# A two-layer graph network with expert FFNs on one core: a list of tile sizes for each layer, and first-layer edge sums placed over 27 of 32 FFN steps

## The chip, the cores and the metric

One core of a Trainium2 chip. The metric is the device time of one execution in microseconds, taken as the median of three runs. One more execution was profiled, and every row below is from it.

## The reference, cut to what matters

There are 6250 nodes of 256 features and 106250 edges sorted by destination node (50000 pairs in both directions and a loop at each node). Four residual steps follow each other:

```python
x = x + gnn0(layernorm(x), edge_weight1)   # mean over in-edges of w*feat[src], [mean, feat] @ W.T + b
x = x + ffn0(layernorm(x))                 # 8 experts, 512 hidden, ReLU, the best 2 by logit
x = x + gnn1(layernorm(x), edge_weight)    # h = relu(xn @ Wp.T + bp); sqrt(sum of w*h[src]**2)
x = x + ffn1(layernorm(x))                 # 8 experts, 256 hidden, GELU, top 2 of a softmax, plus the normed x
```

All four steps are per node, except that each GNN reads rows of arbitrary other nodes. So the first "layer" of the kernel (gnn0 and ffn0) must be through with every node before the second (gnn1 and ffn1) gathers its first row.

## The kernel before, in words

**Tiles.** Nodes are cut into 49 blocks of 128, and the blocks into tiles. `Shape` (line 38) makes one list for both layers: eleven tiles of 4 blocks, then 2, 2 and 1, so 14 tiles. All FFN work of a tile has its 512 (or 256, 128) nodes as the moving columns of the matmul.

**Groups.** Edges come in 208 groups of 512. For a group GpSimd issues four indirect DMAs (L574, `gather_group`), each of which fetches 128 source rows into a ring of SBUF buffers; the ring holds 4 groups in layer 0 and 8 in layer 1, and the gather of group g waits until group g-4 (g-8) has been summed. VectorE makes the one-hot matrices of the group (`onehots`, L1061, L1062; in layer 1 L1066, L1067), TensorE multiplies rows and one-hots into a window of PSUM (`sum_groups`: in layer 0 24 matmuls of L649 and 4 of L653, in layer 1 8 records of L657), and VectorE adds the window to an accumulator in SBUF (`add_windows`, L1091). A tile can be "taken" from the accumulator (`take`) when all its groups have been added. `END[t]` is the number of groups that must be there for tile t; for a full tile there are 17 new ones. The first tile needs 19 groups.

**FFN steps.** A tile goes through M steps, 32 in layer 0 (8 experts of 4 chunks of 128 hidden units) and 16 in layer 1 (8 of 2). Step n on TensorE: `up(n+2)` (6 matmuls, L667), `down(n)` (6 matmuls, L697), and then what is woven in. ScalarE applies the activation (L1432) and makes the high half (L1439), VectorE scales (L1250) and makes the low half (`hidden_low`, L1255, exactly once in each step of each layer, 672 in all). `down(n)` waits for the low half of step n, and in a step with groups also for their one-hots and for the windows of the groups before.

**What is woven in.** At fixed steps of tile t: the results of tile t-1 go back to tokens and, in layer 0, to the table of layer 1 (steps 1 to 12), and tile t+1 is prepared. In layer 0 that is `take` from step 13, features (13), the linear product (18, 19), layernorm and transposes (22), gate logits (24), and the combine weights (29), which `down` waits for in step 30. In layer 1 the same stands at 1, 3, 4, 7, 9 and 13.

**Where the sums go.** `plan` (line 346) writes for each step the groups that are summed in it. The groups of tile t go partly into the last steps of tile t-2, from step `turn` on, and partly into the first `at_take` steps of tile t-1. In layer 0 `turn` is 28 and `at_take` is 13:

```python
early = len(gs) * (self.M - self.turn) // self.M      # 17 * 4 // 32 = 2
late = gs[early:]                                     # 15
```

So in a full tile of layer 0 two groups are summed in steps 28 and 30, fifteen in steps 0 to 12, and none in steps 13 to 27. In layer 1 (`turn` 1, `at_take` 1) one is summed in each of steps 1 to 15 and two in step 0. The groups between the first tile's and the first step's (`begun`) are summed in four places of the first tile's preparation.

**The start of a layer.** GpSimd gathers the groups of tile 0, VectorE finds the largest weight of each matrix between them (`magnitudes`, `at_mags`), GpSimd reduces these over partitions (ahead of group 10), VectorE computes the scales (group 10 in layer 0, 8 in layer 1), and in the groups after these the 16 weight matrices are split into a high and a low half, by ScalarE (L1444) and VectorE (L1003) in turn. Then the tile is taken and prepared, and the first step begins. Layer 1's gathers begin when the last rows of layer 0 are in its table.

Of the kernel before, what the change touches and what calls it, by code (L numbers as in the profile page):

```python
# [5 lines left out]
F32 = mybir.dt.float32  # L6
# [8 lines left out]
P = 128  # L15
D = 256
KD = D // P
NX = 8
# [5 lines left out]
LAG = 2  # L24
WACC = T + 256
# [9 lines left out]
XA = 4  # L35


class Shape:


    def __init__(self, n, e):
        blocks = -(-n // P)
        rest = blocks - 5
        assert rest % SUB == 0 and blocks % XR == 0 and rest >= 4 * SUB
        self.n, self.e = n, e
        self.B = [SUB] * (rest // SUB) + [2, 2, 1]
# [19 lines left out]
def build_program(nc, a, n_nodes, n_edges):  # L66
    sh = Shape(n_nodes, n_edges)
    NT, NG, NPAD, NF = sh.NT, sh.NG, sh.NPAD, sh.NF
    BT, TT, ST, NB, CB, END = sh.B, sh.T, sh.S, sh.NB, sh.CB, sh.END
# [7 lines left out]
    seed0_d = nc.dram_tensor("seed0_d", (NF, P, 3 * T), F32, kind="Internal").ap()  # L77
    seed1_d = nc.dram_tensor("seed1_d", (NF, P, T), F32, kind="Internal").ap()

    def rows(dram, t):  # L80

        return dram[ST[t]:ST[t] + TT[t], :].rearrange("(s p) d -> p s d", p=P)
# [35 lines left out]
    with ctx:  # L118
# [42 lines left out]
        floor_s = sb("floor_s", [P, 2, NG])  # L161
        rel = sb("rel", [P, NG])
        base_i = sb("base_i", [P, NG], I32)
# [60 lines left out]
        chk = aggs[:, :, :].rearrange("p k n -> p (k n)")[:, 0:3 * NG].rearrange("p (a g) -> p a g", a=3)  # L224
# [36 lines left out]
        class Layer:  # L261


            def __init__(self, i):
# [55 lines left out]
                self.i, self.HC = i, (HC0, HC1)[i]  # L320
                self.M = NX * self.HC
# [17 lines left out]
                self.at_mags = ((3, 4, 6, 7), (2, 3, 4, 5))[i]  # L339
                self.at_scales = (10, 8)[i]  # L340
                self.at_reduce = 10

                self.turn = (28, 1)[i]
                self.plan()

            def plan(self):


                steps = [[] for _ in range(self.M * NT + 2)]
                self.begun = [[] for _ in range(4)]  # L350
                for t in range(1, NT):
                    gs = list(sh.groups(t))
                    early = len(gs) * (self.M - self.turn) // self.M
                    late = gs[early:]
                    for k, g in enumerate(gs[:early]):
                        if t == 1:
                            self.begun[k * 4 // early].append(g)
                        else:
                            n = self.turn + k * (self.M - self.turn) // early
                            steps[self.M * (t - 2) + n].append(g)  # L360
# [236 lines left out]
        def _(pe):  # L597
# [167 lines left out]
            def normed_transposed(l, u):  # L765
                pe.wait_ge(l.xn_ready, u + 1)
                for k in range(KD):
                    to_features(xn, u, k, k, l.xnT_summed)
# [837 lines left out]
```

## Time and profile before

| | us |
|---|---|
| median of 3 runs | 3453.04 (3450.09 to 3456.6) |
| the profiled execution | 3462.63 |
| its span, first to last instruction | 3460.8 |
| GpSimd busy (gathers) | 1687.6, 49% of the span |
| TensorE matmul busy | 2546.9, 74% |
| VectorE busy | 1772.4, 51% |
| mean granted TensorE clock | 0.87 of full speed |

The share of busy time is an average over stages that have different limits: the two starts, the FFN steps of layer 0 (from 255 to 2054 us) and those of layer 1 (from 2315 us to the end). A matmul's row has the record's length, and neighbouring matmuls overlap, so the time between two starts is what a sequence costs. A wait whose releaser is "remote" or "issue" is one that the profile can't ascribe.

### The profile page before, as it was taken

The numbers are of one execution on the slowest core, as the hardware profiler recorded it, in microseconds if no ns is written. First come the engines' busy times: TensorE is split into PE (matmuls) and PEld (weight loads), VectorE is DVE, ScalarE is ACT, GpSimd is POOL, SyncE is SP. The second block draws the span as 40 slices with busy tenths as digits, with TensorE's granted clock in tenths as the row PEclk, the third lists the DMA queues.
The fourth block names the chain that finished last, engine by engine and source line by source line (L and its number), as shares of the span: only waits on it lengthen the run. The fifth ranks groups of instructions, "written<-read, shape, count | busy, mean of one in ns | idle before, by whom it ended". The sixth has DMA issues, their size and how long they took to land.

```text
span 3460.8 us, 47385 instructions
## 1 busy us (share of the span) xinstructions
PE 2546.9 (74%) x17983; PEld 1431.0 (41%) x17983; DVE 1772.4 (51%) x4296; ACT 1138.6 (33%) x1835; POOL 1687.6 (49%) x1678
## 2 busy tenths in 40 slices
PE   0147878878787887979798862357778777777897
PEld 0123434434343444434344652334444444444455
DVE  7463645445464545646465642334544444544565
ACT  3022423333232323324244550112332322333355
POOL 3646354352635345263532106666666666666620
PEclk9997989889898988989899985568888898878899
DMA  5523122221313222131311121212222212222110
GB/s 219 174 73 87 58 83 64 72 80 54 98 57 92 62 74 77 58 99 54 91 48 54 35 72 46 54 43 54 58 58 61 59 52 55 59 58 60 52 36 11
DMA packets 115790, 237.80 MB, mean 69 GB/s; under 512 B 30291, under 2 KB 69581, under 8 KB 115045
## 3 DMA queue, kind: packets, MB, share of 16 engines
q0 software_dynamic: 66560, 163.68, 17.0%
q1 hardware_dynamic: 48996, 71.05, 6.1%
q8 instruction: 142, 2.33, 0.3%
q14 instruction: 92, 0.75, 0.1%
HBM read 208.95 MB, written 25.67 MB: 68 GB/s over the span
## 4 chain that ended last, share of the span: by engine, by line
PE 45%; another core or an unknown queue 19%; DVE 15%; issue 13%; ACT 6%; DMA 1%; POOL 1%; DVEq 0%; ACTq 0%; SPq 0%; POOLq 0%
PE psY L697 16%; PE psH L667 15%; PE psM L761 3%; PE psE L657 3%; DVE hsc L1255 3%; PE psE L649 3%; DVE hid L1250 3%; ACT hid L1432 2%; PE psC L674 1%; DVE acc L1091 1%; ACT hsc L1439 1%; PE psM L713 1%; DVE mag L949 1%; ACT L1432 1%
## 5 line engine op out<-in xcount | busy, mean ns | idle before, releaser
L574 POOL DMA_INDIRECT ring<-table,src_s x1664 | 1659.4, 997 | 1575.6 <-PE psE L653 647.6
L697 PE MATMUL psY<-hsc,wbuf 128*128 128x512 f16 (+2 forms) x4032 | 974.6, 377 | 327.9 <-DVE acc L1091 127.5
L667 PE MATMUL psH<-xnT,wbuf 128*128 128x512 f16 (+2 forms) x4032 | 980.6, 381 | 64.3 <-issue 39.4
L1432 ACT ACTIVATE hid<-psH,b,scl 128x512 f32<-128x512 f32 (+2 forms) x672 | 485.8, 723 | 1553.8 <-PE psH L667 868.3
L697 PEld LDWEIGHTS psY<-hsc,wbuf 128*128 128x128 f16 x4032 | 375.6, 102 | 847.7 <-issue 221.9
L1250 DVE TENSOR_TENSOR hid<-hid,psC 128x512 f32<-128x512 f32 (+2 forms) x672 | 415.6, 618 | 557.3 <-ACT hid L1432 384.7
L667 PEld LDWEIGHTS psH<-xnT,wbuf 128*128 128x128 f16 x4032 | 390.4, 105 | 433.2 <-issue 155.9
L1091 DVE TENSOR_TENSOR acc<-acc,psE 128x120 f32 (+1 forms) x416 | 98.3, 236 | 881.4 <-remote 663.0
L1255 DVE TENSOR_TENSOR hsc<-hid,hsc 128x512 f16<-128x512 f32 (+2 forms) x672 | 415.8, 619 | 0.4 <-ACT hsc L1439 0.3
L1439 ACT ACTIVATE hsc<-hid 128x512 f16<-128x512 f32 (+2 forms) x672 | 379.8, 565 | 7.0 <-DVE hid L1250 6.7
L657 PEld LDWEIGHTS psE<-ohbuf,ring 128*128 128x128 f32 x1664 | 264.8, 233 | 52.0 <-DMA ring<-table,src_s 20.2
L657 PE MATMUL psE<-ohbuf,ring 128*128 128x40 f32 x1664 | 255.5, 311 | 26.9 <-DMA ring<-table,src_s 20.0
L649 PE MATMUL psE<-ohbuf,ring 128*128 128x40 f16 x4992 | 178.3, 185 | 67.0 <-issue 35.7
L649 PEld LDWEIGHTS psE<-ohbuf,ring 128*128 128x128 f16 x4992 | 167.4, 100 | 104.6 <-issue 54.8
L624 PE MATMUL psY<-ones_h 128*128 128x1 f16 x86 | 14.9, 186 | 236.1 <-DVE ohbuf L1062 109.4
L674 PE MATMUL psC<-cT,spread 24*128 24x512 bf16 (+2 forms) x224 | 86.2, 385 | 54.9 <-DVE hid L1250 40.7
L624 PEld LDWEIGHTS psY<-ones_h 128*128 128x128 f16 x86 | 10.8, 127 | 242.6 <-DVE ohbuf L1062 110.3
L1444 ACT ACTIVATE wbuf<-wbuf,scl 128x1024 f16<-128x1024 f32 (+1 forms) x32 | 29.9, 935 | 246.6 <-issue 117.3
L1062 DVE TENSOR_TENSOR ohbuf<-ohbuf,wpair 128x320 f16<-128x320 f16 x208 | 102.4, 492 | 7.1
L653 PE MATMUL psE<-ohbuf,ones_h 128*128 128x40 f16 x832 | 62.9, 185 | 43.5 <-issue 43.4
L761 PE MATMUL psM<-gnn_w,featT 128*128 128x256 f32 x294 | 86.8, 406 | 10.2 <-ACT featT L1406 10.2
L1154 DVE TENSOR_TENSOR res<-psM,xin 128x512 f32<-128x512 f32 (+1 forms) x50 | 34.0, 679 | 102.3 <-PE psM L761 70.8
(154 smaller groups left out, 1730.4 us busy)
## 6 DMA issues: line engine op xcount, KB each, us to landing
ring<-table,src_s POOLq DMA_INDIRECT x1664
wbuf<-w_in SPq DMA_DIRECT2D x2, 4096.0 KB, 20.8
wbuf<-x_in SPq DMA_DIRECT2D x7, 896.0 KB, 11.5
table<-ring SPq DMA_DIRECT2D x7, 896.0 KB, 3.6
feat<-table SPq DMA_DIRECT2D x11, 512.0 KB
xin<-x_in SPq DMA_DIRECT2D x11, 512.0 KB
x_d<-x SPq DMA_DIRECT2D x11, 512.0 KB
xin<-x_d SPq DMA_DIRECT2D x11, 512.0 KB
```

The costliest lines, as they stand in the source:

```text
L574: pool.indirect_dma_start(out=l.ring[:, g % l.R, k, :], out_offset=None, in_=l.table, in_offset=bass.IndirectOffsetOnAxis(ap=src_s[:, c:c ...
L649: mm(psE[:, o + h * W:o + (h + 1) * W], l.ring[:, r, k, c:c + P], ohw0[:, q, k, y, :], start=(k == 0 and m == 0), stop=(k == SUB - 1 and m ...
L657: last = mm(psE[:, o:o + W], l.ring[:, r, k, :], ohw1[:, q, k, :], start=(k == 0), stop=(k == SUB - 1))
L667: last = mm(psH[n % 2][:, 0:TT[t]], l.w1(e, i, k, c), x[:, j, k, 0:TT[t]], start=(k == 0 and m == 0), stop=(k == KD - 1 and m == 2))
L674: mm(psC[:, 0:TT[t]], spread[:, e, :], cT[t % 2][0:3 * NX, 0:TT[t]], start=True, stop=True)\
L697: last = mm(psY[d][:, 0:TT[t]], l.w2(e, i, c, d), hsc[n % 2][:, j, 0:TT[t]], start=False, stop=(n == l.M - 1 and m == 2))
L761: last = mm(psM[b][:, (s % 2) * D:(s % 2 + 1) * D], x[:, s * P:(s + 1) * P], w, start=(m == 0), stop=(m == len(parts) - 1))
L1091: tt_(v, v, ps, ALU.add).then_inc(l.window_added, 1)
L1250: tt_(h, h, psC[:, 0:TT[t]], ALU.mult).then_inc(l.hid_scaled, 1)
L1255: tt_(hsc[n % 2][:, 1, 0:TT[t]], hid[n % 4][:, 0:TT[t]], hsc[n % 2][:, 0, 0:TT[t]], ALU.subtract).then_inc(l.hid_lo, 1)
L1432: f(hid[n % 4][:, 0:TT[t]], psH[n % 2][:, 0:TT[t]], (ACT.Relu, ACT.Gelu)[l.i], scale=l.un_up, bias=l.b1[:, n // l.HC, n % l.HC:n % l.HC + ...
L1439: f(hsc[n % 2][:, 0, 0:TT[t]], hid[n % 4][:, 0:TT[t]], ACT.Copy).then_inc(l.hid_hi, 1)
```

## The change

1. Each layer has a `Shape` of its own (`ENDS`). Layer 0 has tiles of 2, 2, 3, nine of 4, 3, 2 and 1 blocks (15 tiles); layer 1 has nine of 4, then 3, 3, 2, 2, 1, 1, 1 (16 tiles). All loops, waits and row ranges go by the layer's own list, and each layer has its own column offsets (`base_i`) for the accumulator.
2. `plan` now gives each allowed step a weight, the tile's columns + 64, and spreads the groups evenly over these weights. The first preparation's four places weigh 1200 each (`LEAD`).
3. In layer 0 `turn` goes from 28 to 18. The steps that may hold sums are then 18 to 31 and 0 to 12, 27 of 32. In layer 1 `turn` stays 1.
4. With 2 blocks, tile 0 of layer 0 needs 11 groups, and so the magnitudes are taken at groups 3 to 6, the reduction comes ahead of group 9, and the 16 matrices are split after the take: 8 before the residual, 4 after it, 4 after the layernorm. Layer 1's start keeps its order.
5. `take` moves the 256 carried columns in pieces when the tile is 1 block. The accumulator check at the start covers both lists.

```diff
+ENDS = (([2, 2, 3], [3, 2, 1]), ([], [3, 3, 2, 2, 1, 1, 1]))
+LEAD = 1200
...
-        self.B = [SUB] * (rest // SUB) + [2, 2, 1]
+        self.B = first + [SUB] * (full // SUB) + last
...
-                self.at_mags = ((3, 4, 6, 7), (2, 3, 4, 5))[i]
+                self.at_mags = ((3, 4, 5, 6), (2, 3, 4, 5))[i]
-                self.at_reduce = 10
-
-                self.turn = (28, 1)[i]
+                self.at_reduce = (9, 10)[i]
+                self.at_split = ((0, 8, 12), (16, 16, 16))[i]
+
+                self.turn = (18, 1)[i]
+                self.early = (0.5, 0.0)[i]
...
+                for t in range(1, self.NT):
+                    turns = self.place(t)
+                    gs = list(self.groups(t))
+                    whole = sum(w for w, _ in turns)
+                    k, passed = 0, turns[0][0]
+                    for i, g in enumerate(gs):
+                        while passed * len(gs) <= (i + self.early) * whole and k < len(turns) - 1:
+                            k += 1
+                            passed += turns[k][0]
+                        n = turns[k][1]
+                        (self.begun[n] if t == 1 and k < 4 else steps[n]).append(g)
...
+            def place(self, t):
+                def step(x):
+                    return self.TT[x] + 64
+                late = [(step(t - 1), self.M * (t - 1) + n) for n in range(self.at_take)]
+                if t == 1:
+                    return [(LEAD, k) for k in range(4)] + late
+                return [(step(t - 2), self.M * (t - 2) + n) for n in range(self.turn, self.M)] + late
...
                 for _ in take(l, 0):
                     pass
+                for k in range(l.at_split[0], l.at_split[1]):
+                    matrix_low(l, k)
...
                 for _ in residual(l, 0):
                     pass
+                for k in range(l.at_split[1], l.at_split[2]):
+                    matrix_low(l, k)
                 begin(1)
                 normed(l, 0)
                 normed_low(l, 0)
+                for k in range(l.at_split[2], 2 * NX):
+                    matrix_low(l, k)
```

By this plan the groups of a full tile of layer 0 stand in the steps as follows (a dot is a step without a sum, "2" a step with two; steps 0 to 31):

```
before  2 1 1 1 1 1 2 1 1 1 1 1 1 . . . . . . . . . . . . . . . 1 . 1 .
after   . 1 1 . 1 1 . 1 . 1 1 . 1 . . . . . 1 . 1 1 . 1 . 1 1 . 1 1 . 1
```

In layer 0 the groups summed within the steps of a tile are now 11, 13, 18, 18, 17 (six times), 15, 11, 4, 1 and 0, where before they were 17 (nine times), 16, 9, 7, 2 and 0. In layer 1 they are 17 in each of the first seven tiles, then 14, 13, 8, 9, 4, 4, 2, 0, 0, where before they were 17 in each of the first nine tiles and then 10, 8, 2, 1 and 0.

## Rows read from the trace of the kernel before

**Rows 1.** The page: the span, and GpSimd busy in tenths of 40 slices.

```profile
span 3460.8 us, 47385 instructions
...
POOL 3646354352635345263532106666666666666620
```

**Rows 2.** Stretch, length, busy time of L1255 (its count), PEclk, DMA share, GB/s.

```profile
254.70:1774.70 1520.00, 219.50 (x320) 0.90 0.25 72
...
868.30:951.10 82.80, 8.95 (x13) 0.88 0.34 99
951.10:970.80 19.70, 3.42 (x5) 0.91 0.30 93
970.80:1018.90 48.10, 9.57 (x14) 1.00 0.08 24
...
1774.70:1828.90 54.20, 8.94 (x13) 0.97 0.29 85
1828.90:1843.00 14.10, 3.42 (x5) 1.00 0.23 68
1843.00:1884.80 41.80, 9.57 (x14) 1.00 0.07 20
1884.80:1963.80 79.00, 13.35 (x32) 0.94 0.18 51
1963.80:2019.60 55.80, 13.35 (x32) 1.00 0.03 11
```

**Rows 3.** Stretches of layer 0: PE, PEld, DVE, ACT, POOL busy (instructions), PEclk, DMA share, GB/s.

```profile
868.30:951.10 82.80, 61.49 (x609) 31.19 (x608) 35.28 (x83) 21.90 (x34) 55.16 (x55) 0.88 0.34 99
...
970.80:1018.90 48.10, 47.57 (x295) 25.28 (x294) 33.10 (x77) 21.63 (x35) 5.74 (x6) 1.00 0.08 24
1774.70:1828.90 54.20, 47.18 (x410) 24.27 (x409) 28.81 (x65) 22.00 (x34) 30.34 (x30) 0.97 0.29 85
```

**Rows 4.** Waits within steps 0 to 12 of the fifth tile: total, times, longest.

```profile
DVE acc L1091 <- remote: 26.6, 6, 6.7
...
POOL ring L574 <- issue: 14.3, 47, 0.3
```

**Rows 5.** The page, section 5: the gather instructions.

```profile
L574 POOL DMA_INDIRECT ring<-table,src_s x1664 | 1659.4, 997 | 1575.6 <-PE psE L653 647.6
```

**Rows 6.** TensorE in order of time, in a quiet step with one sum.

```profile
1008.75 0.76 PE L649 MATMUL psE<-ohbuf,ring 128*128 128x40 f16 x24
...
1009.45 1.46 PE L667 MATMUL psH<-xnT,wbuf 128*128 128x512 f16 x6
```

**Rows 7.** VectorE in order of time, the start of layer 0.

```profile
163.19 0.28 DVE L1091 TENSOR_TENSOR acc<-acc,psE 128x120 f32 x1 [8.13 <-remote]
...
209.94 1.28 DVE L1003 SCALAR_TENSOR_TENSOR wbuf<-wbuf,scl 128x1024 f16<-128x1024 f32 x1
212.44 1.28 DVE L1003 SCALAR_TENSOR_TENSOR wbuf<-wbuf,scl 128x1024 f16<-128x1024 f32 x1 [1.22 <-ACT wbuf L1444]
...
216.64 3.91 DVE L1110 RECIPROCAL acc<-acc 128x128 f32<-128x128 f32 x4
```

**Rows 8.** As rows 2, layer 1: the fourth tile, and the eighth to the last.

```profile
2620.00:2721.00 101.00, 10.97 (x16) 0.84 0.22 57
...
3025.60:3230.60 205.00, 21.88 (x32) 0.82 0.21 57
3230.60:3306.30 75.70, 10.97 (x16) 0.95 0.19 50
3306.30:3362.90 56.60, 10.93 (x16) 1.00 0.13 35
3362.90:3402.00 39.10, 6.67 (x16) 1.00 0.06 19
3402.00:3438.40 36.40, 6.67 (x16) 0.95 0.03 9
3438.40:3454.50 16.10, 4.55 (x16) 1.00 0.06 18
```

More of the change, by code:

```diff
@@ L35, with __init__ @@
 XA = 4
+LEAD = 1200
 class Shape:
-    def __init__(self, n, e):
+    def __init__(self, n, e, layer):
         blocks = -(-n // P)
-        rest = blocks - 5
-        assert rest % SUB == 0 and blocks % XR == 0 and rest >= 4 * SUB
+        first, last = ENDS[layer]
+        full = blocks - sum(first) - sum(last)
+        assert full % SUB == 0 and blocks % XR == 0 and full >= 4 * SUB and last[-1] == 1
         self.n, self.e = n, e
-        self.B = [SUB] * (rest // SUB) + [2, 2, 1]
+        self.B = first + [SUB] * (full // SUB) + last
         self.NT = len(self.B)
@@ L346, in plan @@
             def plan(self):
-                steps = [[] for _ in range(self.M * NT + 2)]
+                steps = [[] for _ in range(self.M * self.NT + 2)]
                 self.begun = [[] for _ in range(4)]
[L351 to L360, printed above, removed]
-                    for k, g in enumerate(late):
-                        steps[self.M * (t - 1) + k * self.at_take // len(late)].append(g)
@@ L514, in _ @@
                     general_store(l)
-                    sp.wait_ge(L[0].out_stored, 16 * NT)
-                    sp.wait_ge(s_hTw, 16 * NT)
+                    sp.wait_ge(L[0].out_stored, 16 * L[0].NT)
+                    sp.wait_ge(s_hTw, 16 * L[0].NT)
                 inputs(l, 0)
                 seed_load(l, 0)
-                for t in range(NT):
-                    last = t == NT - 1
+                for t in range(l.NT):
+                    last = t == l.NT - 1
                     if not last:
@@ L709, in back_to_tokens, with to_features @@
                     last.then_inc(l.ytok_summed, 1)
-            def to_features(src, t, b, k, then):
-                for s in range(BT[t]):
+            def to_features(l, src, t, b, k, then):
+                for s in range(l.BT[t]):
                     last = pe.transpose(psM[b][:, s * P:(s + 1) * P], src[:, s, k * P:(k + 1) * P],
@@ L787, in _ @@
                 general_sums(l)
-                for g in sh.groups(0):
+                for g in l.groups(0):
                     sum_first(l, [g])
@@ L806, in _ @@
                 up(l, 0, 1)
-                for t in range(NT):
-                    last = t == NT - 1
+                for t in range(l.NT):
+                    last = t == l.NT - 1
                     for n in range(l.M):
@@ L1102, in take @@
                     hold(dve)
-                wait(dve, l.lin_summed, CB[u])
+                wait(dve, l.lin_summed, l.CB[u])
                 if l.i == 0:
@@ L1317, in _ @@
                 scale(l, 0, 0)
-                for t in range(NT):
-                    last = t == NT - 1
+                for t in range(l.NT):
+                    last = t == l.NT - 1
                     taking = adding = weighing = None
@@ L1478, in _ @@
                 act.wait_ge(l.scales_ready, 1)
-                for k in range(2 * NX):
+                for k in range(l.at_split[0]):
                     matrix_high(l, k)
@@ L1489, in _ @@
                 active(l, 0, 0)
-                for t in range(NT):
-                    last = t == NT - 1
+                for t in range(l.NT):
+                    last = t == l.NT - 1
                     for n in range(l.M):
@@ L1588, in laid_out @@
         "partmask": partmask.reshape(9 * NX, 3),
-        "floor": np.tile(floor, (P, 1, 1)),
+        "floor": np.tile(floor, (P, 1, 1, 1)),
     }
```

270 lines of the change are left out of this document (142 added, 128 removed).

## The prediction, made blind

> **What bounds the kernel now.** I read the page first. Its GpSimd line is the odd one [rows 1]: in the left half the digits go up and down, 5 2 3 5 3 4 5 2, and in the right half they stand at 6. So in layer 1 the gathers run all the time, and in layer 0 they come in bursts, one to a tile. Next I cut the FFN of layer 0 at the starts of L1255, which VectorE issues once a step, so that a count of 32 is a tile [rows 2]. Ten full tiles take 1520 us, 152 each. Within one of them (the fifth) the 13 steps that hold 15 sums take 82.8 us, 6.4 a step; the next 5 take 19.7, and the last 14, with 2 sums, take 48.1, 3.4 a step.
>
> Is that difference the work of the sums? One sum holds TensorE for 1009.45 - 1008.75 = 0.70 us [rows 6]. Thirteen more of them are 9 us, and the difference is far more. The view of all engines says what the rest is [rows 3]. In steps 18 to 31 TensorE is busy 47.6 of 48.1 us at full clock: it is the bound there, and nothing is to be had but its work. In steps 0 to 12 it is busy 61.5 of 82.8 us, at a clock of 0.88, so 21 us of a tile are lost idle and more in slow matmuls. In the waits, VectorE's additions of windows stand idle 26.6 us there, six times, up to 6.7 us at once, by a releaser that the profile can't name [rows 4], and `down` waits for these additions.
>
> The best witness is the eleventh tile. It has 4 blocks like the others, but 8 sums in steps 0 to 12. These steps take 54.2 us in place of 82.8 [rows 2]: seven sums fewer, 28.6 us less, **4.1 us a sum**, six times its work of 0.70. And TensorE's idle time there is 54.2 - 47.2 = 7.0 us, 0.9 for each of 8 sums [rows 3]. So a sum costs 0.70 + 0.9 = 1.6 us when they stand thin and 4.1 at the margin when they stand dense. Why dense ones cost more is plain in part: a gather instruction takes 1.0 us and leaves 0.3 us of gap [rows 4, 5], so a group costs GpSimd 5.2 us, and the ring holds 4. Fifteen groups in 82.8 us are one in 5.5 us: GpSimd runs at its limit, 55.2 us busy plus 0.3 us of gap for each of 55 instructions, and then it has nothing to do for the rest of the tile (5.7 of 48.1 us [rows 3]).
>
> **The change part by part.** My sum is made against the profiled execution, 3462.6 us with a span of 3460.8 [rows 1]; the median of the runs is 9.6 us lower, and I take that off at the end.
>
> *The placing of sums in layer 0.* In a full tile there are now 8 sums in steps 0 to 12, as in the eleventh tile: 54.2 us. Steps 13 to 17 have none and were 14.1 us there; features of 4 blocks in place of 2 make it 14.6. Steps 18 to 31 were 48.1 us with 2 sums and get 9: 7 x 0.70 = 4.9 of work, and 0.9 idle for each of 9, 8 us: 61. Together **130 us, 22 less than 152**. Groups then come one in 130/17 = 7.6 us, well over 5.2, so GpSimd has 30% to spare, where the ring can fill again in steps 13 to 17. Moved past VectorE and GpSimd are also the one-hots (two instructions) and the window additions of seven groups a tile; VectorE is busy 33 of 48 us there [rows 3] and gets 7 x 1.1 = 8 more, which fits but is no longer roomy. Bounds for a late sum's idle time: 0 (TensorE's work alone, tile 122) and 4.1 - 0.7 = 3.4 (as in the dense steps, tile 153). I take 0.9, since its steps are as thinly filled as those of the row.
>
> *The small tiles at the start of layer 0.* The first tile's take moves from 19 groups to 11. Group 10 is added at 163.2 us, and the matrices' splits now come after the take. Before, one is done every 2.5 us (209.94 to 212.44), the take begins at 216.6 [rows 7] and the first step is at 254.7 [rows 2], 38 us later. After: 163, a take of 5 us for 2 blocks, 16 splits x 2.5 = 40, and the chain from residual to first step, some 28 us for half the columns: 236, **19 us earlier**. But these tiles are short against their groups. A 2-block tile takes 55.8 us with 2 sums and 79.0 with 7, 4.6 us a sum [rows 2], because GpSimd is again at its limit. Tiles 0 to 2 get 11, 13 and 18 sums. I take 3.0 a sum for the 2-block ones, between 1.6 and 4.6, and 2.0 for the 3-block one, which is slower by itself: 52 + 9 x 3.0 = 79, 56 + 11 x 3.0 = 89, 80 + 18 x 2.0 = 116. So the 7 blocks end at 236 + 284 = 520 us. Before, 7 blocks end at 254.7 + 1.75 x 152 = 521. The early start is given back; bounds 490 and 545.
>
> *The rest of layer 0.* The tile after these has 18 sums: 132. Six of 17: 780. One with 15: 127. The last full one has 11 and a smaller one behind it: 110 [rows 2] + 2 x 1.6 + 2 = 116. Then 84 (3 blocks, 3/4 of a full one's work and 4 sums), 55 and 35, as now. 520 + 132 + 780 + 127 + 116 + 84 + 55 + 35 = 1849, where layer 0 now ends at 2054: **205 us less**.
>
> *Layer 1.* Its start and first seven tiles keep their groups and order. There 17 groups take 101.0 us [rows 8], one in 5.9 us, near GpSimd's limit; the pair of sums moves from step 0 to 1, which I cost at nothing, as the ring of 8 hides it. If that cover is gone it is a wait for one group, up to 5 us a tile. From the eighth tile on it now takes 205.0 + 75.7 + 56.6 + 39.1 + 36.4 + 16.1 = 429 us [rows 8]. The new tiles by the same rows, with (101.0 - 75.7)/7 = 3.6 us a group at 4 blocks: 90 and 85 (14 and 13 groups), 52 and 52 (3 blocks: between 42, three quarters of 56.6, and 57), 43 and 42 (2 blocks with 4 groups), 28, 27 and 16. Here 28 is 16.1 plus the 11 us by which a 2-block tile with a successor (39.1) is longer than half a 4-block one (28.3): the preparation's chain doesn't shrink with the tile. Sum 435, **6 us more**; bounds -20 and +25. Three tiles more also mean three times the fixed instructions, which are in these rows.
>
> The new instructions at the start (lists of 2 x 208, one cast more) are a few of under 1 us beside loads that GpSimd waits for anyway: 0 to 2 us.
>
> Sum: 3462.6 - 205 + 6 = 3263, less 9.6: **about 3252 us**.
>
> **The rivals.** *The idle time follows the sum, not its density.* Then a tile stays at 152, and only start and ends count. For it: layer 1, with a sum in every step, loses as much as the dense steps of layer 0. Against: the eleventh tile, 54.2 against 82.8 us. It would give 520 + 8 x 152 + 130 + 84 + 55 + 35 = 2040 for layer 0, 3448 profiled, about 3440. Chance 0.12.
>
> *The late sums break the next tile's preparation (slower).* Steps 18 to 31 hold the chain linear product, layernorm, logits, combine weights, which TensorE meets in order and for which `down` waits in step 30. Now nothing disturbs it. If each late window addition stalls VectorE by the 4.4 us of [rows 4] (26.6/6) and TensorE stands still for it, these steps take 48 + 5 + 9 x 4.4 = 93, the tile 162 us, 10 more than now, and the kernel 3440 + 8 x 10 = 3520. It decides from 3.4 us a late sum on. For it: the stalls have no cause that I can see in the trace. Against: 7.0 us idle for 8 sums in the eleventh tile. Chance 0.05.
>
> *GpSimd's instructions get longer beside a busier VectorE.* Gathers now overlap steps 18 to 31 too, where VectorE is 69% busy (33.1 of 48.1 us) against 43% in the dense steps. If each gather waited out one L1255 of 0.69 us (8.95/13 [rows 2]), a group would cost 5.2 + 2.8 = 8.0 us, a full tile at least 17 x 8.0 = 136 and with its waits some 142, the kernel 3350. Against: the six gathers there take 0.96 us each (5.74/6), the 55 of the dense steps 1.00 [rows 3]. Chance 0.05. The Trainium skill has this as a rule: by the GPSIMD Engine Reference (its table of figures, SBUF interfaces) GpSimd shares these with VectorE and contends with instructions of two SBUF inputs, as L1255 is. The trace doesn't show that here.
>
> *Better than the sum.* Fewer gaps keep the clock at 1.00 and late sums cost only their work: 122 a tile, and 490 for the first three. That is 3252 - 64 - 30 = 3158 or less. Chance 0.06.
>
> That the change doesn't do what it says I exclude: the places follow from the plan, as written out.
>
> **How the numbers follow.** The forecast holds with 0.72, from tiles of 125 to 143 us. I predict 3252. Eight tiles at 143 add 104, the start's 25 and layer 1's 20 seldom come together with it: the upper end is 3375. The lower is 3252 - 40 - 30 - 20 = 3162. Outside are the first two rivals and most of the last, 0.2 together. A difference within 0.2%, 7 us, is about what a measurement of this kernel can't tell from none. Faster by more: 0.94. Slower: 0.05, the second rival. Same: 0.01, a corner of the first.
>
> **What would show it.** Steps 0 to 12 of a middle tile of layer 0 near 54 us and steps 18 to 31 near 61; GpSimd's digits in layer 0 even, at 6; TensorE's clock there 0.95 or more; the first L1255 near 236 us and layer 0's last near 1849; from the eighth tile of layer 1 to the end 435 us. I am wrong if steps 18 to 31 take over 75 us, or if the gathers wait in them for nothing but the ring while TensorE is idle.

## The result, and the profile after

The changed kernel takes 3301.17 us (median of 4 runs, 3294.23 to 3310.41), the kernel before 3451.57 beside it (3449.07 to 3456.6): a ratio of **0.9564, interval 0.9536 to 0.9592**. That is 150 us less, where 200 were forecast; 3301 lies within the range of 3162 to 3375. The profiled execution took 3297.65 us.

The page after (GpSimd and granted clock by slice; the gathers; the window additions), which answers to [rows 1, 5]:

```profile
span 3295.9 us, 49574 instructions
...
POOL 3635555454454454544520076666666666665510
PEclk9969999999999999999999855588787888899998
...
L591 POOL DMA_INDIRECT ring<-table,src_s x1664 | 1652.1, 993 | 1413.6 <-issue 630.5
...
L1110 DVE TENSOR_TENSOR acc<-acc,psE 128x120 f32 (+1 forms) x416 | 98.5, 237 | 674.3 <-remote 476.5
```

GpSimd's digits in layer 0 no longer swing between 2 and 5; they stand at 4 and 5, not at 6 as forecast: by the prediction's own numbers 68 gathers of 1.0 us in a tile of 130 us are 0.52. Line numbers have moved by 17 to 27: the gathers are L591 (were L574), the window additions L1110 (L1091), the scaling that ends an FFN step L1276 (L1255).

Busy time by stage, cut where L1276 ends: to the first FFN step; the three small tiles; the rest of layer 0; to layer 1's first step; its first tile; the next six; the eighth to the last. The columns are those of [rows 3].

```profile
0.00:236.60 236.60, 32.48 (x512) 26.11 (x512) 142.37 (x305) 53.06 (x71) 101.40 (x88) 0.89 0.43 152
236.60:542.30 305.70, 240.14 (x2533) 169.03 (x2533) 170.63 (x457) 109.52 (x231) 168.20 (x166) 0.93 0.29 85
542.30:1868.40 1326.10, 1207.00 (x10038) 657.47 (x10037) 825.92 (x1877) 556.19 (x951) 593.24 (x593) 0.98 0.26 75
1868.40:2120.70 252.30, 83.17 (x416) 72.27 (x414) 74.77 (x211) 21.14 (x34) 161.01 (x166) 0.53 0.23 67
2120.70:2225.30 104.60, 77.00 (x369) 43.09 (x367) 45.97 (x124) 29.75 (x42) 66.58 (x69) 0.81 0.19 51
2225.30:2841.50 616.20, 490.48 (x2390) 270.96 (x2388) 296.33 (x781) 195.56 (x277) 402.61 (x409) 0.82 0.21 57
2841.50:3289.20 447.70, 358.50 (x2514) 233.63 (x2514) 248.01 (x776) 219.39 (x401) 187.26 (x192) 0.92 0.15 42
```

Against before, layer 0 gives nearly all: its first step ends 19 us earlier and its FFN takes 1631.8 us where it took 1798.6. Layer 1 gives some back: its first seven tiles take 720.8 us where they took 705.3, and from the eighth tile on it is 447.7 us where it was 432.9.

One full tile of layer 0 (the sixth), in steps 0 to 12, 13 to 17 and 18 to 31, beside [rows 3]:

```profile
806.30:858.70 52.40, 47.57 (x409) 24.42 (x409) 28.93 (x66) 22.03 (x36) 29.35 (x30) 0.97 0.30 87
858.70:873.70 15.00, 14.83 (x104) 7.37 (x105) 11.87 (x18) 6.87 (x11) 6.61 (x7) 1.00 0.39 120
873.70:940.40 66.70, 55.84 (x466) 29.85 (x464) 40.58 (x96) 21.64 (x35) 31.88 (x32) 0.97 0.25 72
```

The view of the waits says what TensorE still waits for: line waited at, releaser, total, times, longest.

```profile
DVE acc L1110 <- remote: 476.5, 149, 30.9
ACT hid L1459 <- remote: 337.0, 96, 16.1
POOL ring L591 <- remote: 242.3, 123, 6.0
```

Before, the additions had 663.0 us of it, 145 times. "Remote" is a releaser that the profile can't name. The timeline of one such wait shows more:

```profile
820.53 0.26 PE L670 MATMUL psE<-ohbuf,ones_h 128*128 128x40 f16 x4
...
821.57 1.02 POOL L591 DMA_INDIRECT ring<-table,src_s  x1 [0.30 <-issue]
...
823.60 0.78 ACT L1459 ACTIVATE hid<-psH,b,scl 128x512 f32<-128x512 f32 x1 [3.89 <-PE psH L684]
823.62 0.28 DVE L1110 TENSOR_TENSOR acc<-acc,psE 128x120 f32 x1 [1.85 <-remote]
...
824.23 1.24 POOL L591 DMA_INDIRECT ring<-table,src_s  x1 [1.65 <-remote]
```

TensorE's last matmul of the sum ends at 820.79, and neither VectorE nor GpSimd goes on before 823.62 and 824.23. By the code L1110 waits for the sum alone, and VectorE's instruction ahead of it ended at 821.77. Nothing but TensorE's own signal is missing: it comes **2.8 us late**, just after a burst of four gathers (the last ends at 822.59), and ScalarE, waiting for a matmul group that ended at 822.09, starts at the same moment. The Trainium skill (Perfetto Trace Analysis, Tensor Engine Instruction) tells that the update travels after the end that the profile reports, and gives no time for it. Here it is long.

The trace also records when a semaphore is raised, and this settles whose signal is late. The semaphore of layer 0's sums is raised at 823.49, 2.70 us after the end at 820.79. Of the 208 sums of layer 0, 118 are announced over 1 us after their end in this trace and 118 in the trace of before; the mean of these is 2.5 us after and 3.8 us before. In e1, at the faster level, the median is 0.013 us. It is TensorE's signals alone: in this trace 557 of its updates come 0.5 to 8 us after the end that the trace has for it, of ScalarE's none and of VectorE's one, and in the five kernels of the faster level with all gathers TensorE has one each.

### The profile page after: what moved, and what is told of

It is laid out like the page before. It is cut to its first block, busy times and chain, and to the rows that moved or that the text cites. A ratio compares the mean times of both kernels' runs of the same rounds, so it can differ in the third digit from the quotient of the medians.

```text
span 3295.9 us, 49574 instructions
## 1 busy us (share of the span) xinstructions
PE 2489.7 (76%) x18773; PEld 1473.1 (45%) x18773; DVE 1804.4 (55%) x4526; ACT 1185.3 (36%) x2007; POOL 1680.3 (51%) x1678
## 4 chain that ended last, share of the span: by engine, by line
PE 40%; DVE 23%; another core or an unknown queue 19%; issue 9%; ACT 6%; DMA 1%; POOL 1%; DVEq 1%; ACTq 0%; SPq 0%; POOLq 0%
PE psY L714 15%; PE psH L684 12%; DVE hsc L1276 4%; DVE hid L1271 4%; PE psE L674 3%; PE psM L778 3%; ACT hid L1459 2%; PE psE L666 2%; DVE acc L1110 1%; PE psC L691 1%; DVE ohbuf L1081 1%; DVE wbuf L1022 1%; DVE mag L968 1%; ACT L1459 1%
## 5 line engine op out<-in xcount | busy, mean ns | idle before, releaser
L591 POOL DMA_INDIRECT ring<-table,src_s x1664 | 1652.1, 993 | 1413.6 <-issue 630.5
L714 PE MATMUL psY<-hsc,wbuf 128*128 128x512 f16 (+3 forms) x4416 | 962.3, 355 | 292.2 <-DVE hsc L1276 162.8
L684 PE MATMUL psH<-xnT,wbuf 128*128 128x512 f16 (+3 forms) x4416 | 955.9, 354 | 26.7 <-issue 25.3
L1459 ACT ACTIVATE hid<-psH,b,scl 128x512 f32<-128x512 f32 (+3 forms) x736 | 508.4, 691 | 1286.4 <-PE psH L684 840.1
L1271 DVE TENSOR_TENSOR hid<-hid,psC 128x512 f32<-128x512 f32 (+3 forms) x736 | 425.6, 578 | 560.3 <-ACT hid L1459 372.1
L684 PEld LDWEIGHTS psH<-xnT,wbuf 128*128 128x128 f16 x4416 | 418.5, 104 | 347.3 <-issue 97.0
L1110 DVE TENSOR_TENSOR acc<-acc,psE 128x120 f32 (+1 forms) x416 | 98.5, 237 | 674.3 <-remote 476.5
L1276 DVE TENSOR_TENSOR hsc<-hid,hsc 128x512 f16<-128x512 f32 (+3 forms) x736 | 425.7, 578 | 0.3 <-ACT hsc L1466 0.3
L1466 ACT ACTIVATE hsc<-hid 128x512 f16<-128x512 f32 (+3 forms) x736 | 392.7, 534 | 8.9 <-DVE hid L1271 7.8
L674 PEld LDWEIGHTS psE<-ohbuf,ring 128*128 128x128 f32 x1664 | 265.5, 234 | 54.5 <-DMA ring<-table,src_s 22.8
L691 PE MATMUL psC<-cT,spread 24*128 24x512 bf16 (+3 forms) x248 | 91.0, 367 | 65.4 <-DVE hid L1271 53.5
L691 PEld LDWEIGHTS psC<-cT,spread 24*128 24x128 bf16 x248 | 22.8, 92 | 163.5 <-issue 83.0
L778 PE MATMUL psM<-gnn_w,aggs 128*128 128x256 f32 x294 | 85.1, 399 | 3.4 <-ACT aggs L1426 1.5
```

Source lines behind the costliest of these rows:

```text
L591: pool.indirect_dma_start(out=l.ring[:, g % l.R, k, :], out_offset=None, in_=l.table, in_offset=bass.IndirectOffsetOnAxis(ap=src_s[:, c:c ...
L674: last = mm(psE[:, o:o + W], l.ring[:, r, k, :], ohw1[:, q, k, :], start=(k == 0), stop=(k == SUB - 1))
L684: last = mm(psH[n % 2][:, 0:l.TT[t]], l.w1(e, i, k, c), x[:, j, k, 0:l.TT[t]], start=(k == 0 and m == 0), stop=(k == KD - 1 and m == 2))
L691: mm(psC[:, 0:l.TT[t]], spread[:, e, :], cT[t % 2][0:3 * NX, 0:l.TT[t]], start=True, stop=True)\
L714: last = mm(psY[d][:, 0:l.TT[t]], l.w2(e, i, c, d), hsc[n % 2][:, j, 0:l.TT[t]], start=False, stop=(n == l.M - 1 and m == 2))
L778: last = mm(psM[b][:, (s % 2) * D:(s % 2 + 1) * D], x[:, s * P:(s + 1) * P], w, start=(m == 0), stop=(m == len(parts) - 1))
```

## The experiments

The runs met two levels of time: in two sets the kernel before takes 2971 and 2973 us, in two others 3479 and 3449, as in the first result. The same code ran on different chips there (two at the faster level, and at least two at the slower), so a ratio is only taken within a set. The unnamed waits stand in every trace of the 3450 level that keeps all gathers and in none of the 2970 level. The table has what L1276's ends give (L1255 in a kernel before), in us; "full tile" is the mean of those with 17 groups, "rest" is layer 1 from its eighth tile on. The rows without a ratio are single executions; the stage columns are of the profiled execution, "time" is the median.

| | level | time | ratio | L0 first step | full tile | L0 end | L1 first step | first seven | rest |
|---|---|---|---|---|---|---|---|---|---|
| before | 3450 | 3451.6 | 1 | 255.5 | 152 | 2054.1 | 2315.9 | 705.3 | 432.9 |
| after | 3450 | 3301.2 | 0.9564 | 236.6 | 131.9 | 1868.4 | 2120.7 | 720.8 | 447.7 |
| e6, before | 3450 | 3487.9 | | 256.1 | 152.6 | 2061.5 | 2325.7 | 715.0 | 438.6 |
| e7, turn 23 | 3450 | 3403.3 | 0.9795 | 272.0 | 146.6 | 1985.2 | 2243.3 | 713.0 | 438.3 |
| e8, placing and new start | 3450 | 3287.7 | 0.9442 | 301.9 | 132.1 | 1880.0 | 2149.4 | 719.1 | 431.9 |
| e5, changed | 3450 | 3315.1 | 0.9524 | 234.1 | 131.2 | 1869.2 | 2133.6 | 718.3 | 455.4 |
| e1, placing | 2970 | 2842.3 | 0.9573 | 234.5 | 113.5 | 1623.8 | 1829.3 | 610.1 | 394.9 |
| e2, turn 28 | 2970 | 2979.0 | 1.0034 | 218.5 | 122.9 | 1750.1 | 1956.4 | 606.0 | 399.4 |
| e3, old list in L1 | 2970 | 2861.2 | 0.9630 | 219.2 | 113.5 | 1640.6 | 1847.0 | 609.7 | 398.1 |
| e9, list 2 ... 2, 1 | 2970 | 2850.7 | 0.9586 | 224.7 | 113.5 | 1633.2 | 1838.0 | 608.7 | 395.0 |
| e10, turn 14 | 2970 | 2841.3 | 0.9554 | 233.4 | 113.7 | 1624.1 | 1830.3 | 607.7 | 394.0 |
| e4, before, 1 gather | 2970 | 2566.5 | | 212.0 | 113.8 | 1605.5 | 1734.1 | 473.5 | 350.4 |
| e11, changed, 1 gather | 2970 | 2623.1 | | 200.7 | 113.3 | 1618.2 | 1749.6 | 474.3 | 390.7 |
| e12, as e8, 1 gather | 3450 | 2579.9 | | 232.5 | 113.4 | 1617.6 | 1749.4 | 474.4 | 347.2 |

### e1 to e4: the parts of the change

e1 keeps the new placing and takes lists and start back:

```diff
-ENDS = (([2, 2, 3], [3, 2, 1]), ([], [3, 3, 2, 2, 1, 1, 1]))
+ENDS = (([], [2, 2, 1]), ([], [2, 2, 1]))
-                self.at_mags = ((3, 4, 5, 6), (2, 3, 4, 5))[i]
+                self.at_mags = ((3, 4, 6, 7), (2, 3, 4, 5))[i]
-                self.at_reduce = (9, 10)[i]
+                self.at_reduce = 10
-                self.at_split = ((0, 8, 12), (16, 16, 16))[i]
+                self.at_split = (16, 16, 16)
```

> Both lists of tiles and the start are those of before; only the placing of the sums is the new one (turn 18, even weights). Theory A, the gain is the placing in layer 0: full tiles take 131 us in place of 152, nine or ten of them, so 3453 - 200 = about 3255 us, faster than the whole change (3301), since the three small tiles at the start and the longer end of layer 1 each cost some 15 to 20 us. Theory B, the gain needs the small tiles at the start (19 us earlier first step): not better than 3301, about 3310 to 3320.

2842.28 us, 0.9573 [0.9557, 0.9589]. The view of a full tile (the fifth), in the same three stretches, and the page's window additions and chain by line:

```profile
685.40:729.80 44.40, 44.33 (x406) 23.76 (x407) 29.06 (x66) 21.64 (x34) 31.58 (x33) 1.00 0.38 115
729.80:745.30 15.50, 15.50 (x109) 7.66 (x107) 11.83 (x19) 7.83 (x13) 7.58 (x7) 1.00 0.37 119
745.30:798.90 53.60, 52.81 (x466) 29.80 (x464) 40.37 (x96) 21.43 (x35) 29.53 (x29) 1.00 0.26 79
```

```profile
POOL ring L591 29%; PE psY L714 17%; PE psH L684 15%; PE psE L666 4%; PE psM L778 4%; DVE hsc L1276 2%; DVE hid L1271 2%; DMA ring<-table,src_s 1%; ACT hid L1459 1%; PE psC L691 1%; PE psM L730 1%; DVE xn L1162 1%; PE psM L738 1%; PE psE L670 1%; ACT L1421 1%
...
L1110 DVE TENSOR_TENSOR acc<-acc,psE 128x120 f32 (+1 forms) x416 | 98.1, 236 | 389.1 <-PE psE L674 302.9
```

TensorE is busy 112.6 of 113.5 us at full clock: nothing of the idle time is left, with the same 17 sums. So a thinly placed sum costs no idle time here; e2 has the dense ones. GpSimd's gathers make 29% of the whole chain, and 61.5% of it in layer 1 from 1829 us on, where every step has its sum. And no addition waits for a remote signal. Neither theory's time came, since both were worked out for the other level, and the whole change wasn't run at this one.

e2 is the changed kernel with the old turn, 28 for 18:

```diff
-                self.turn = (18, 1)[i]
+                self.turn = (28, 1)[i]
```

> The changed kernel with turn back at 28 in layer 0: 17 sums of a tile in 17 steps, none in steps 13 to 27; lists and start as changed. Theory A (density): full tiles are back at 150 us, eight of them at 18 us more, so about 3301 + 145 = 3445 us. Theory B (lists and start): at most 3350.

2978.98 us, 1.0034 [1.0018, 1.0049]: lists and start without the placing bring nothing. The even weights stay, so steps 0 to 12 hold 13 sums where before they held 15. A full tile:

```profile
729.50:784.00 54.50, 48.41 (x519) 25.85 (x517) 33.91 (x81) 21.78 (x34) 41.30 (x44) 1.00 0.40 120
784.00:803.00 19.00, 16.92 (x138) 8.59 (x139) 12.33 (x20) 7.83 (x13) 14.23 (x16) 1.00 0.47 146
803.00:852.20 49.20, 48.64 (x324) 26.18 (x323) 35.31 (x81) 21.51 (x34) 10.02 (x10) 1.00 0.13 38
```

In steps 0 to 12 GpSimd has 41.3 us of gathers and 0.3 of gap behind each of 44: 54.5 of 54.5 us. There it is the bound, and it costs 122.9 - 113.5 = 9.4 us a tile. So idle time goes with density, not with the sum.

e3 is the changed kernel with layer 1's old list:

```diff
-ENDS = (([2, 2, 3], [3, 2, 1]), ([], [3, 3, 2, 2, 1, 1, 1]))
+ENDS = (([2, 2, 3], [3, 2, 1]), ([], [2, 2, 1]))
```

> The changed kernel with layer 1's tiles back at eleven of 4, then 2, 2, 1. If the three extra small tiles cost what the trace of after shows (447.7 us from the eighth tile on against 432.9 before), this is 15 us faster than the changed kernel, about 3286. If the smaller tiles help, because less work is left behind the last gather, it is slower, 3310 or more.

2861.16 us, 0.9630 [0.9614, 0.9646], 19 us slower than e1, which has the old list and start in layer 0 too. The two differ at the start (first e3: to the first step, the next 7 blocks, the rest of layer 0; then e1):

```profile
0.00:219.20 219.20, 33.55 (x512) 26.63 (x512) 143.09 (x305) 52.80 (x71) 103.01 (x88) 0.88 0.46 165
219.20:454.30 235.10, 215.53 (x2535) 160.54 (x2533) 171.12 (x458) 110.50 (x231) 161.47 (x163) 1.00 0.37 109
454.30:1640.60 1186.30, 1165.17 (x10038) 655.41 (x10037) 825.72 (x1877) 559.24 (x951) 603.24 (x595) 1.00 0.28 84
```

```profile
0.00:234.50 234.50, 55.06 (x878) 42.81 (x878) 160.19 (x346) 55.71 (x72) 136.55 (x126) 0.96 0.52 180
234.50:429.60 195.10, 191.04 (x1666) 103.46 (x1667) 137.18 (x289) 82.41 (x129) 123.91 (x124) 1.00 0.34 101
429.60:1623.80 1194.20, 1168.38 (x10158) 664.52 (x10156) 830.20 (x1911) 564.95 (x972) 600.22 (x596) 1.00 0.28 84
```

The first step comes 15.3 us earlier, the next 7 blocks take 40.0 longer, the end list gets 7.9 back: 16.8 us lost. Of the 40, TensorE's own work is 24.5: it now does in the FFN the sums that it did before the first step (22 us less there), and 40 more steps of fixed cost (3 tiles for 1.75).

e4 is the kernel before with one gather of four, which cuts GpSimd's work and leaves TensorE's:

```diff
-                for k in range(SUB):
+                for k in range(1):
-                    pe.wait_ge(l.gathered[g % l.R], 16 * SUB * (g // l.R + 1))
+                    pe.wait_ge(l.gathered[g % l.R], 16 * (g // l.R + 1))
-                                    mm(psE[:, o + h * W:o + (h + 1) * W], l.ring[:, r, k, c:c + P],
+                                    mm(psE[:, o + h * W:o + (h + 1) * W], l.ring[:, r, 0, c:c + P],
```

(and the same in layer 1's matmul). All matmuls, one-hots and additions are in place, but the sums are of other rows, so that what is computed differs; the same holds for e11 and e12.

> The kernel before with one gather to a group in place of four; each group's sums read the one block four times, so aggregates are of other rows, and three quarters of the gathering is left out. Everything else, the dense placing of the sums too, is as it was. If the dense steps are slow because GpSimd gathers at its limit, steps 0 to 12 of a full tile of layer 0 fall from 82.8 to about 60 us (15 sums x 1.6 + 35) and a full tile from 152 to about 130. If they are slow because TensorE and VectorE are crowded by the sums themselves, steps 0 to 12 stay over 75 us. The unnamed waits of up to 30 us at layer 1's start (first gather to first step 246 us) either vanish too (GpSimd's activity makes them) or stay.

2566.52 us, full tile 113.8 with the sums as dense as ever: density of sums as such costs nothing. It is the density of gathers; their issue by GpSimd and their transfers are cut together here, so these two are not told apart.

### e5 to e8: the same at the level of the first result

e5 is the changed kernel as it is, e6 the kernel before with a profile.

> The changed kernel as it is, beside the kernel before on one chip, so that the parts can be read against the whole. Theory (the placing alone brings the gain, the list of the first layer costs some 17 us net, the list of the second layer nothing): where the kernel before takes 2971 us, 2861 with a ratio of 0.963, layer 1 from its first step to its end 1005 to 1008 as with the old list. Rival (the list of layer 1 costs what the first chip's two traces showed, 15 us from its eighth tile on): 2876. Rival (the list of layer 1 brings something): below 2855. On a chip where the kernel before takes 3451, 3301 and a ratio of 0.956 as first measured.

3315.11 us, 0.9524 [0.9499, 0.9549]. The rest of layer 1 takes 455.4 us, where e6, e7 and e8 have 438.6, 438.3 and 431.9 with the old list. At this level the list of layer 1 costs 17 to 24 us there (15 between the first two traces); at the other (e2 against e1 and e3) 1 to 5.

> The kernel before, profiled on the chip of the experiments. Theory (even there the first layer is held up where the sums are dense, and nowhere else): a full tile of layer 0 takes 123 to 125 us, its steps 0 to 12 some 55 to 57 and its steps 18 to 31 some 48 to 50; the tile with 17 groups in its steps 0 to 12 has TensorE waiting for gathered rows there. Rival (what the placing brought there is something else than density, such as an earlier first step): a full tile near 114 us already, and a first step later than 250.

The expectation was worked out for the other level (its 123 to 125 us come from there), and neither its theory nor its rival gives what came. Here the tile is 152.6 us, as in the first trace. Steps 0 to 12 of the fifth tile:

```profile
861.20:941.90 80.70, 58.59 (x575) 30.86 (x572) 35.59 (x85) 21.56 (x33) 52.97 (x53) 0.83 0.32 94
```

GpSimd: 53.0 us of gathers and 53 gaps of 0.3 are 69 of 80.7 us. It is **not** at its limit, unlike in e2. What holds both back is a third thing, the late signals: the additions wait 699.8 us for a remote one in this trace.

e7 is e1 with turn 23 for 18.

> The new way of placing alone (old tile lists, old start), with the early sums from step 23 on instead of 18, so that 22 of 32 steps carry the 18 sums and not 27. Theory of a queue (GpSimd issues gathers at about 5.2 us a group and the ring of four holds what it has ahead; with turn 28 the 17 sum steps of e2 took 67 us for 18 groups; 22 steps take 74 us of TensorE's own, so the gathers fit): no loss against turn 18, full tile 113.5, 2842 us, 0.957. Rival (each step of higher density costs its share, half way between turn 28 and turn 18): full tile 118, 2885 us, 0.971.

3403.29 us, 0.9795 [0.9758, 0.9832], full tile 146.6. That is faster than before; whether by 2% the interval leaves open. It ran at the 3450 level, where the queue's arithmetic doesn't hold, and no loss was wrong. Nor is it the rival's half way: five more steps with sums (17 to 22 of 32) bring 6.0 us a tile, the next five (to 27, e8) 14.5. Its first step comes at 272.0, though the start is the old one: the new placing sums seven groups between the first tile's and the first step where before there were two. From the first tile's last sum to the first step it is 54 us here and 37 in e6.

e8 is e1's lists with the changed start, that is the changed kernel with

```diff
-ENDS = (([2, 2, 3], [3, 2, 1]), ([], [3, 3, 2, 2, 1, 1, 1]))
+ENDS = (([], [2, 2, 1]), ([], [2, 2, 1]))
```

> The new way of placing with the old tile lists in both layers, but with the changed start of layer 0: splits of the weights moved behind the first tile's groups (0, 8, 12 for 16, 16, 16) and magnitudes and scales one group earlier. It parts the two things that could have made the first FFN step 15.3 us earlier with the small first tile. Theory (the small first tile brings it, through fewer groups to gather and sum before the first step): first step 234 to 240, time 2842 to 2848, 0.957 to 0.959. Rival (the order of the splits brings it): first step 220 to 225, full tiles of 113.5 from the first on, 2828 us, 0.952.

3287.73 us, **0.9442 [0.9414, 0.9469]**, 27 us better than the changed kernel in the same set. The first step is at 301.9 us, later than both expected, in the profiled run, which is the slowest of its four (3278.6 to 3309.4), so that the two profiled executions lie 6 us apart and not 27. In them layer 0 ends 10.8 us later in e8, and the rest of layer 1 takes 23.5 less. With a first tile of 4 blocks the new split order doesn't bring an earlier first step: e7, with the same placing and the old order, has 272.0. No run has a small first tile with the old order.

### e9 to e12

e9 puts one small tile ahead in place of one at the end.

```diff
-ENDS = (([2, 2, 3], [3, 2, 1]), ([], [3, 3, 2, 2, 1, 1, 1]))
+ENDS = (([2], [2, 1]), ([], [2, 2, 1]))
```

> The changed placing and start with the tile lists 2, eleven of 4, 2, 1 in layer 0 and the old list in layer 1: the small tile stands ahead in place of one at the end. Theory (an early first step is worth what the small first tile brings, and only the small tiles behind it, which carry the gathers of full ones, give it back): where the kernel before takes 2971, first step near 219, first tile 59 to 70, full tiles 113.5, end of layer 0 at 1612 to 1624, time 2831 to 2843 (0.953 to 0.957); where it takes 3451 to 3479, first step near 235, full tiles 130 to 133, ratio 0.940 to 0.950. Rival (each block in a small tile costs as much as it brings at the start, wherever it stands): 2855 to 2862 (0.961 to 0.963), or on the other chip as the changed kernel, 0.952 to 0.956.

2850.73 us, 0.9586 [0.957, 0.9602]. Between the two, and the theory falls: the full tiles behind it are 113.5 us, but the first tile takes 81.6, not 59 to 70. It carries 14 sums and 62 gathers: 59.5 us of gathers and 16.1 of gaps, 75.6 of 81.6, so GpSimd is near its limit there. Layer 0 ends at 1633.2, 9.4 later than in e1. A small tile ahead doesn't pay even alone.

e10 is e1 with turn 14 for 18.

> The new way of placing alone (old tile lists, old start) with the early sums from step 14 on, so that 31 of 32 steps carry the sums. Theory of two regimes: where the kernel before takes 2971 us, TensorE was already the bound at turn 18, so nothing is left to win: full tile 113.5, 2842, 0.956 to 0.958. Where it takes 3451 to 3479, the full tile went 152, 141 to 149, 130 to 135 with 17, 22 and 27 of 32 steps filled, so it goes on with the density: 124 to 128, 0.930 to 0.942. Rival (there each sum costs its stall whatever the spacing from 27 steps on): full tile 130 to 133, 0.944 to 0.950.

By the code its sums of steps 14 to 17 fall among the steps at which acc is divided and shifted for the next tile, so that what is computed differs; all instructions are in place. It met the 2970 level: 2841.29 us, 0.9554 [0.9538, 0.957], full tile 113.7. As expected there, nothing is left to win by more spreading. Whether it would win at 3450 wasn't seen.

e11 is the changed kernel with e4's edit.

> The changed kernel with one gather for each group where there are four; the sums read the one gathered block four times, so that three of four rows' contributions to each sum are those of the first (that part of the computation is changed), with all matmuls, one-hots and additions in place. Theory (what is above TensorE's own time comes from GpSimd's gathers and the signals that wait beside them): no named or unnamed wait of note in layer 0, full tile 113.5, first three tiles 57, 57 to 62 and 84 to 88, time 2570 to 2590 on either chip. Rival (on the chip where the kernel before takes 3451 to 3479 the late signals have nothing to do with GpSimd's work): full tile 125 to 133 still, and waits of VectorE's additions for a remote signal as before, time over 2900.

2623.08 us, 33 above the theory, and 57 above e4, though the full tile is 113.3. The first three tiles take 60.9, 75.6 and 95.4 us, as in e3 with all gathers (60.9, 75.7, 98.4): the small tiles cost TensorE's side, not gathers (it is busy 56.9, 66.2 and 91.7 us of them in e11). So does layer 1's list, from the eighth tile on (first e11, then e4):

```profile
2223.90:2614.60 390.70, 342.33 (x2519) 230.46 (x2516) 247.41 (x775) 220.28 (x401) 46.78 (x48) 0.96 0.08 24
```

```profile
2207.60:2558.00 350.40, 322.71 (x2123) 199.65 (x2121) 231.21 (x647) 187.56 (x309) 49.33 (x49) 1.00 0.09 27
```

40 us, half of it TensorE's work. With all gathers it is 1 to 5 at the 2970 level. The likely reason is that GpSimd is the bound there and hides most of it.

e12 is e8 with e4's edit.

> The new way of placing and the changed start with the old tile lists, and one gather for each group where there are four, the sums reading the one block four times (the part of the computation that is changed). Whichever chip it meets, it tells two things. Without gathers to wait for, placing should be worth nothing: full tile of layer 0 113.5 to 114 as in e4, end of layer 0 1390 to 1395 after its first step, where e4 stood at 1393.5. The first step tells the changed start by itself: theory (the order of the splits does little, 212 of e4 give or take 4); rival (it brings most of what the first step gained): 200 or less. Where the kernel before takes 3451 to 3479, the late signals are tried too. Theory (they come with GpSimd's gathers): waits of VectorE's additions for a remote signal, 496 us in the changed kernel, fall to a quarter or less, full tile 113.5 to 117, time 2570 to 2650. Rival (they have nothing to do with the gathers): 400 us or more of such waits, full tile 125 or more.

It met the 3450 level (before 3449.44) and took 2579.89 us. The page's gathers and additions, and a full tile's steps 0 to 12:

```profile
L591 POOL DMA_INDIRECT ring<-table,src_s x416 | 434.8, 1045 | 1907.3 <-PE psE L670 1138.3
...
L1110 DVE TENSOR_TENSOR acc<-acc,psE 128x120 f32 (+1 forms) x416 | 98.2, 236 | 161.8 <-PE psE L674 80.7
```

```profile
680.00:724.40 44.40, 44.35 (x407) 23.76 (x407) 29.00 (x67) 21.77 (x34) 9.19 (x8) 1.00 0.14 43
```

No wait for a remote signal is left among the waits, none of the 208 sums of layer 0 is announced over 1 us late (118 after), and the stretch is e1's to 0.02 us of TensorE. **With three of four gathers gone the two levels are one**: the late signals come with the gathers. The tile is e4's, too (113.4 and 113.8), so placing is worth nothing without gathers to wait for.

The first step is at 232.5, where e4 with the old start has 212.0; neither theory. In e12 the splits stand behind all of the first tile's sums; VectorE in order of time, the take and the first and the last split:

```profile
155.13 0.28 DVE L1110 TENSOR_TENSOR acc<-acc,psE 128x120 f32 x1 [1.82 <-PE psE L670]
155.73 0.49 DVE L1126 TENSOR_SCALAR acc<-acc,wscl 128x512 f32<-128x512 f32 x1 [0.32 <-DVE acc L1110]
163.98 1.28 DVE L1022 SCALAR_TENSOR_TENSOR wbuf<-wbuf,scl 128x1024 f16<-128x1024 f32 x1
...
213.37 1.28 DVE L1022 SCALAR_TENSOR_TENSOR wbuf<-wbuf,scl 128x1024 f16<-128x1024 f32 x1 [1.22 <-ACT wbuf L1471]
```

In e4 the last split starts at 174.3, between additions. So in e12 the first tile's sums are through 19 us earlier, and from there to the first step it takes 77 us where e4 takes 38. Not all of this is the splits: e12 sums 26 groups before its first step and e4 21, as the new placing puts seven and not two behind the first tile's. The two runs are also of different levels, so the 20 us can't be put down to the order of the splits to the last one; that the splits stand in that stretch, 16 of 2.5 us each, is plain.

## Why the prediction was right, and what in it was off

**The placing.** Right, and the largest term. A full tile was forecast at 130 and is 131.9: in the six with 17 groups steps 0 to 12 average 52.3 (54.2), 13 to 17 15.3 (14.6), 18 to 31 64.4 (61). The last were priced 3.4 too low and the first 1.9 too high, and the two cancel in part. e1 and e2 show that it is the placing that gives it. All of layer 0 behind the small tiles was 1329 in the sum and is 1326.1.

**The mechanism behind it** was only half right. The prediction had GpSimd at its limit in the dense steps, 55.2 us and 0.3 for each of 55. That is 71.7 of 82.8 us, not the limit. The runs part the 152 us of a tile: 113.5 of TensorE's work (e1, e12), 9.4 for GpSimd's limit at turn 28 (e2), and some 29 for late signals of TensorE beside dense gathers, of which about 18 are left after (131.9 - 113.5). The 9.4 and the 29 are an estimate: they take from one level what was measured at the other, where 13 sums and not 15 stood in steps 0 to 12, and no run parts them at 3450. The 4.1 and 1.6 us a sum held although their reason was incomplete, since they were read from the eleventh tile of the same trace, which had the late signals in it. That is a sound way to a price, and no proof of the mechanism.

**The small tiles at the start.** The first step came to 0.6 us (236), and that is luck. The sum was 163 + 5 + 40 + 28. The last of the 11 groups was added at 173.2, ten later; 5 us passed to the first split; the splits ended at 224.1, 45.5 us for 40, because part of the preparation now stands between them; and for the same reason only 12.5 of the chain's 28 were left behind them. The 2 + 2 + 3 blocks were the term mis-sized: 75.9, 99.0 and 130.7 us for 79, 89 and 116, 305.7 for 284. At the other level the same three take 235.1 (e3), so about 71 of the 305.7 go with the late signals. "The early start is given back" was put at nothing net, and it is a loss: 17 us at 2970 (e3 against e1). At 3450 no run has the lists apart from the start. The prices were 3.0, 3.0 and 2.0 us a sum, chosen between 1.6 and 4.6; by the same bases they came out at 2.7, 3.9 and 2.8. And the reason given for the 4.6, that GpSimd is again at its limit in the two-block tile of 79.0 us, misreads the trace. GpSimd works only in the first half of that tile and is busy 20.2 us in the whole of it (columns of [rows 3]):

```profile
1884.80:1925.30 40.50, 29.77 (x344) 22.69 (x343) 19.03 (x58) 14.71 (x31) 20.17 (x20) 0.87 0.31 85
```

TensorE has 65.3 us of work there and 51.8 in the tile of 55.8 us, 13.5 more, of which five sums of 0.70 are 3.5. Even with one gather of four that tile takes 69.8 us (e4). Much of the 4.6 was other work than sums.

**Layer 1.** "6 us more" is 14.8 (447.7 for 432.9), and 17 to 24 in the set of e5 to e8. The sum had the fixed instructions of three more tiles "in these rows"; e11 shows 40 us of cost by itself, of which the gathers seem to hide some. The pair of sums moved from step 0 to 1 cost nothing, as put: tiles 2 to 7 take 616.2 for 615.8. The first tile took 15.1 more and the way to the first step 9.5 less; at 2970 that way is 204.8 to 206.4 us in all five kernels with full gathers, and here 252 to 269 in six traces, so it goes with the level and its late signals, and a gain of this change isn't shown in it.

**The median.** 9.6 us were taken off the profiled execution; this time the median lies 3.5 above it. So 3297.65 - 3263 = 35 us are in the terms above (19 in layer 0, 9 in layer 1's end, 6 in the two stretches that vary) and 13 in this.

**The rivals.** That idle time follows the sum is refuted by e1 and e4. Late sums that break the preparation (steps 18 to 31 over 75 us) didn't come: 64.4, at most 66.7. GpSimd's gathers didn't get longer by the 0.69 us of that rival: 31.88/32 = 1.00 us in steps 18 to 31. But a little of it is there. In this trace a gather that starts while an L1276 runs takes 1.08 us and another one 0.98; in e1 it is 1.12 and 0.98. The rule of the Trainium skill (GPSIMD Engine Reference, SBUF interfaces) agrees with the trace in its direction; the size is 0.1 us for such a gather. "Better than the sum", 122 a tile, is what the 2970 level exceeds (113.5) and this one doesn't reach.

What stays open: why TensorE's signals come late beside gathers at one level and never at the other, and what the changed kernel as a whole takes at 2970 (it wasn't run there; an estimate from e3, whose layer 1 is as long as e2's to 3 us, is near 2861).

## What to carry to other kernels

Spread what an in-order queue must feed over all the steps that can take it: the same 17 sums cost 9 to 39 us a tile packed in 17 steps and 0 to 18 in 27. Price a moved step by a stretch of the same trace that already has the new density, not by a mechanism. Tiles ramped at the ends cost their fixed steps, and a small tile beside a large one carries the large one's groups; here the placing and the new start with the old lists beat the whole change (0.9442 against 0.9524, e8 and e5), and at the other level the placing alone beats the change with layer 1's old list (0.9573 against 0.9630, e1 and e3).

## What the runs showed of the hardware

The same kernel takes 2971 and 2973 us on two chips and 3449 to 3479 on others. The difference is in no engine's own instructions (gathers of 989 to 997 ns at the slower level and 984 to 1005 at the faster, the additions 236 or 237 ns) but in TensorE's signals, which arrive late: after, 476.5 us of remote waits at the additions, none in the five kernels at 2970. TensorE's clock is lower with it (0.89 after, 0.94 in e1). The difference vanishes with the gathers: 2566.5 us (e4, faster level) and 2579.9 (e12, slower level) for two kernels with one gather of four. This kernel, with its many small indirect gathers beside TensorE, has to be compared on one chip.
